# A two-layer transformer block on one core: layer two's queries and keys turned so that features lie on partitions, its output product from f16 parts

## What is computed

```
xn = layernorm(x)
x = x + attn0(xn) + ffn0(xn)     # 32 query heads of 8 over 8 key heads, causal, rotary; fp8 gated GELU, hidden 1024
xn = layernorm(x)
x = x + attn1(xn) + ffn1(xn)     # below; ternary weights, gated SiLU, rms norm, hidden 1024

def attn1(x):                    # 16 heads of 16; B=2, S=1024
    q, k, v = (x @ w.T).reshape(b, s, 16, 16) for w in (wq, wk, wv)
    q, k = apply_rope(q), apply_rope(k)       # pairs (even, odd) -> (x1 cos - x2 sin, x1 sin + x2 cos)
    scores = einsum('bshd,bstd->bsht', q, k) / 4      # among the 16 heads of ONE token
    attn = einsum('bsht,bstd->bshd', softmax(scores), v)
    return attn.reshape(b, s, 256) @ wo.T
```

## Time and profile before

| | |
|---|---|
| device time, median of 3 runs | 564.69 us (564.24 to 565.04) |
| the profiled execution | 564.45 us |
| its span in the trace | 562.7 us |
| mean granted clock of TensorE | 0.982 of full |
| busy: TensorE, its weight loads | 518.6 us (92%), 256.9 us |
| busy: ScalarE, VectorE, GpSimd | 468.0 (83%), 391.0 (69%), 234.7 us (42%) |
| DMA | 214396 packets, 46.05 MB; 40.5% of 16 engines' span on SP's queue |

### The profile page before, as it was taken

The page is one execution under the profiler, slowest core; times in us unless marked ns, Lnnn a source line. Parts: engine busy times, 40 slices in busy tenths (PEclk is TensorE's granted clock), DMA queues, the critical chain, the costliest instruction groups (busy, mean ns, idle before and its releaser), DMA issues.

```text
span 562.7 us, 12411 instructions
## 1 busy us (share of the span) xinstructions
PE 518.6 (92%) x4661; PEld 256.9 (46%) x4705; DVE 391.0 (69%) x845; ACT 468.0 (83%) x607; POOL 234.7 (42%) x302
## 2 busy tenths in 40 slices
PE   2489789999999999999999999999999999998885
PEld 1123334333444555545545454564454443455563
DVE  5756798977868678767788965748454455577673
ACT  2389999999999999999899889989898888963450
POOL 2576856443452257152765764044244210351100
PEclk9869999999999999999999999999999999999997
DMA  8923210311353516241421725455344253247853
GB/s 272 284 62 99 57 24 11 73 40 40 47 91 48 103 36 94 62 76 29 77 51 45 128 49 79 85 82 96 75 90 66 53 85 66 68 70 132 125 105 94
DMA packets 214396, 46.05 MB, mean 82 GB/s; under 512 B 197440, under 2 KB 213056, under 8 KB 214336
## 3 DMA queue, kind: packets, MB, share of 16 engines
q1 hardware_dynamic: 213760, 44.93, 40.5%
q10 hardware_dynamic: 576, 0.33, 0.4%
HBM read 19.02 MB, written 10.49 MB: 52 GB/s over the span
## 4 chain that ended last, share of the span: by engine, by line
PE 77%; DMA 6%; DVE 4%; ACT 4%; SPq 3%; issue 3%; POOL 2%; DVEq 0%; ACTq 0%
PE psV L706 23%; PE psS L692 8%; PE psA L875 3%; PE psC L782 3%; PE psS L828 3%; PE psC L875 3%; ACT Pt L958 2%; PE psB L875 2%; PE psB L885 2%; PE psA L885 2%; PE psB L839 2%; PE psA L782 2%; PE psA L743 2%; PE psB L743 2%; PE psC L743 1%
## 5 line engine op out<-in xcount | busy, mean ns | idle before, releaser
L958 ACT ACTIVATE Pt<-psS 128x1024 f32<-128x1024 f32 x288 | 280.1, 1031 | 24.0 <-PE psS L692 19.2
L706 PE MATMUL psV<-Pt,vaug 128*32 128x512 f32 x1152 | 149.8, 605 | 1.8 <-POOL Pt L1633 1.4
L1633 POOL TENSOR_SCALAR_AFFINE_SELECT Pt<-Pt 128x1024 f32<-128x1024 f32 x64 | 71.6, 1143 | 75.7 <-ACT Pt L958 75.5
L692 PE MATMUL psS<-qTf,kTf 32*128 32x512 f16 x576 | 65.8, 388 | 4.8 <-ACT Pt L958 3.1
L692 PEld LDWEIGHTS psS<-qTf,kTf 32*128 32x128 f16 x576 | 17.9, 91 | 84.2 <-ACT Pt L958 51.4
L1683 POOL TENSOR_TENSOR ss<-ss,mhalf 128x1 f32<-128x1 f32 x16 | 9.6, 597 | 87.0 <-DVE ss L1470 87.0
L706 PEld LDWEIGHTS psV<-Pt,vaug 128*32 128x32 f32 x1152 | 25.4, 108 | 42.7 <-issue 34.7
L1016 ACT ACTIVATE stage<-psS 128x1024 f32<-128x1024 f32 x32 | 31.0, 1023 | 7.0 <-PE psS L828 6.9
L1624 POOL TENSOR_TENSOR QXf<-rt,QXf 128x512 f16<-128x512 f32 x16 | 19.9, 1242 | 27.4 <-ACT QXf L945 27.4
L1304 DVE SCALAR_TENSOR_TENSOR gw<-gw,gb 128x512 f32<-128x512 f32 x32 | 27.6, 866 | 4.8 <-ACT gw L973 4.8
L1613 POOL TENSOR_TENSOR rt<-qkv,cs 128x320 f32<-128x320 f32 x16 | 16.1, 1003 | 27.4 <-DVE qkv L1189 19.8
(11 more groups left out here) (353 smaller groups left out, 1113.1 us busy)
## 6 DMA issues: line engine op xcount, KB each, us to landing
qkvscr<-rqkv SPq DMA_DIRECT2D x16, 384.0 KB, 2.7
G<-qkvscr SPq DMA_DIRECT2D x24, 128.0 KB, 3.8
stage<-in_wg SPq DMA_DIRECT2D x4, 512.0 KB, 8.2
w8g<-qkvscr SPq DMA_DIRECT2D x16, 128.0 KB, 3.6
oscr<-o SPq DMA_DIRECT2D x16, 128.0 KB, 3.2
at<-oscr SPq DMA_DIRECT2D x16, 128.0 KB, 2.5
out<-yout SPq DMA_DIRECT2D x16, 128.0 KB, 2.3
x<-in_x SPq DMA_DIRECT2D x1, 1536.0 KB, 12.3
```

The lines of the kernel that those rows point to most:

```text
L692: e.matmul(psS[j], kd[32 * j:32 * j + k, h, 128 * at:128 * at + 128], qd[32 * j:32 * j + k, 4 * h:4 * h + 4, :].rearrange("p s n -> p (s n ...
L706: ins = e.matmul(psV[32 * j:32 * j + 32, :], vaug[:, at, j, 32 * h:32 * h + 32], Pt[(4 * Q + j) % NP], start=(kb == 0 and h == 0), stop=(k ...
L958: e.activation(flat(Pt4[:, u % NP:u % NP + 2, :]), flat(psS4[:, j:j + 2, :]), ACT.Exp, scale=scale).then_inc(S["exp"], 1)
L1633: e.affine_select(out=p, in_=p, pattern=[[0, 8], [1, 128]], compare_op=ALU.is_ge, fill=0.0, base=0, channel_multiplier=-1).then_inc(S["mas ...
```

## The change

Queries and keys of layer two are computed with features on partitions, and stay so; the turn into groups goes through DRAM in the turned form.

- The columns of wq and wk are put in another order on the host (`turn`): first the even members of the rotary pairs of q and k, then the odd ones, each with (pair, head) as its 128 features. `qkv1.2n` has the weights as the stationary operand: 4 x 6 products of 128x128 weights with 128 tokens.
- The rotation takes tables with tokens along the free dimension (`turns`): `sin` writes them on ScalarE (two more activations of 1024 columns), `tT.0` to `tT.3` turn them on TensorE, `tTc.0` to `tTc.4` copy them. `rab` (DVE) multiplies straight from PSUM, `rr` (POOL) adds and subtracts. `qk1c`, `ro1`, `ro1p`, `ro2` leave the first pass.
- `rw` writes queries and keys to DRAM (two DMAs, runs of 8 values), `rd` reads them as S1 needs them (four DMAs of 16 partitions). The rows that hide other tokens are loaded once (`mk`). `gT`, `gTq`, `gTk` leave the first pass. `vw` and `vr` carry the values alone.
- `ow` writes in 1 KB runs, `at1r` gathers 64 B pieces. `a1p` (DVE) splits the result in f16 high and low parts, `aq` turns it by a DMA transpose, `wo1` is six f16 products of 256 columns. `at1T` and `at1Tc` leave the first pass; `yo` scales.
- The gating weights are loaded two to `stage`, two to `stmp`, the latter from ScalarE's queue; x from tile 4 on is loaded in three parts from there; the other weights follow later (`lc`, `lw`).
- Some buffers share one (`big`). The range checks take in the new values.
- All five lists of `ORDER` are new.

```diff
+            def mk(k):
+                w.wait_ge("tc", 0 if k else 12)
+                for s in range(2):
+                    dst = (qk1Todd if k else qk1T)[:, s, :, :].rearrange("p j n -> p (j n)")
+                    for b in range(4):
+                        e.dma_start(dst[32 * b + 16:32 * b + 24, :], A["ind2"][s]).then_inc(S[f"d_rd{k}"], 16)
+            def rw(n):
+                src = flat(rqkv[n % 2][:, 0:2, :]).rearrange("p (f m a) -> p f m a", f=2, a=8)
+                dst = rscr[n].rearrange("b s j (f i) (h a) -> f (i h) (b s j) a", f=2, a=8)
+                for f in range(2):
+                    w.wait_ge("rr", 2 * n + f + 1)
+                    e.dma_start(dst[f], src[:, f, :, :]).then_inc(S[f"d_rw{n % 2}"], 16)
+            def rd(n):
+                w.wait_ge(f"d_rw{n % 2}", 32 * (n // 2 + 1))
+                w.wait_ge(f"d_rd{n % 2}", 128)
+                w.wait_ge("S1", 4 * (n - 1))
+                for b in range(4):
+                    dst = (qk1Todd if odd(n) else qk1T)[32 * b:32 * b + 16, :, :, :].rearrange("p s j n -> p (s j) n")
+                    e.dma_start(dst, rscr[n, b].rearrange("s j d n -> d (s j) n")).then_inc(S[f"d_rd{n % 2}"], 16)
+            def aq(n):
+                w.wait_ge("a1p", 2 * n + 2)
+                w.wait_ge("wo1", n + 1 - len(at1q))
+                e.dma_start_transpose(at1q[n % len(at1q)], at1p).then_inc(S["d_aq"], 16)
...
+                    if part == 0:
+                        for c in range(4):
+                            for k, (pt, q, a) in enumerate(((0, 0, 0), (1, 0, 0), (0, 1, 0), (0, 0, 1), (1, 0, 1), (0, 1, 1))):
+                                ins = e.matmul(bank[:, 128 * c:128 * c + 128], wparts[:, q, a, 128 * c:128 * c + 128],
+                                               src[:, pt, 128 * a:128 * a + 128], start=(k == 0), stop=(k == 5))
+                        ins.then_inc(S["qkv1"], 1)
...
+                    for k, (pt, q, a) in enumerate(((0, 0, 0), (0, 1, 0), (0, 0, 1), (0, 1, 1), (1, 0, 0), (1, 0, 1))):
+                        ins = e.matmul(bank[:, 0:256], src[:, 2 * pt + a, :], wo1parts[:, q, a, :], start=(k == 0), stop=(k == 5))
+                    ins.then_inc(S["wo1"], 1)
...
+                e.activation(turns[:, 2, :].rearrange("p (m h) -> p m h", h=16),
+                             ang[:, 0, :].unsqueeze(2).to_broadcast([128, 64, 16]), ACT.Sin)
+                e.activation(turns[:, 1, :].rearrange("p (m h) -> p m h", h=16),
+                             ang[:, 2, :].unsqueeze(2).to_broadcast([128, 64, 16]), ACT.Sin, bias=hpi[:],
...
+            def rab(n):
+                bank = psM[filled["qkv1", 2 * n] % len(psM)][:].rearrange("p (e s t) -> p e s t", e=2, s=2)
...
+                for k in range(2):
+                    e.tensor_tensor(r1[:, k, :].rearrange("p (e s t) -> p e s t", e=2, s=2), bank,
+                                    turns[:, k:k + 2, t0:t0 + 128].unsqueeze(2).to_broadcast([128, 2, 2, 128]),
+                                    ALU.mult).then_inc(S["rab"], 1)
...
+                e.tensor_scalar(at1p[:, 0:256], at1[0][:], OUP, None, ALU.mult).then_inc(S["a1p"], 1)
+                w.wait_ge("a1p", 2 * n + 1)
+                e.scalar_tensor_tensor(at1p[:, 256:512], at1[0][:], OUP, at1p[:, 0:256], ALU.mult,
+                                       ALU.subtract).then_inc(S["a1p"], 1)
...
+            def rr(n):
+                dst = flat(rqkv[n % 2][:, 0:2, :])
+                w.wait_ge("rab", 2 * n + 2)
+                w.wait_ge(f"d_rw{n % 2}", 32 * (n // 2))
+                for f, op in enumerate((ALU.subtract, ALU.add)):
+                    e.tensor_tensor(dst[:, 256 * f:256 * f + 256].rearrange("p (b s j a) -> p s b j a", b=4, s=2, j=4),
+                                    by_group(r1[:, f, 0:256]), by_group(r1[:, f, 256:512]), op).then_inc(S["rr"], 1)
```

More of the change, by code:

```diff
@@ L191 @@
 QUAD_STAGES = {"pe": ("qk", "pv"), "act": ("exp",), "pool": ("mask",)}
-AGAIN = {"sp": [("wg", k) for k in range(6, 12)], "pool": [("zf", 0)] + [("w8a", k) for k in range(6)],
-         "dve": [step for k in range(6) for step in (("w8m", k), ("w8s", k))]}
+AGAIN = {"sp": [("wg", k) for k in range(6, 12)], "pool": [("zf", 0), ("gz2", 0)] + [("w8a", k) for k in range(6)],
+         "dve": [("cst", 0)] + [step for k in range(6) for step in (("w8m", k), ("w8s", k))]}
 def one_round(engine, n):
@@ L225 @@
     "wo0": lambda n: ("xa", n + 1), "up": lambda m: ("fh" if m % 2 else "g", m // 2 + 1), "down": lambda n: ("yff", n + 1), "flagT": lambda n: ("flag", 1), "wsum": lambda m: ("wmin", m + 1),
-    "xn1T": lambda n: ("xn1f", n - NT + 1), "qkv1": lambda m: ("v1c" if m % 2 else "qk1c", m // 2 + 1),
-    "gT": lambda m: ("gTk" if m % 2 else "gTq", m // 2 + 1), "gTagain": lambda n: ("gTm", n - NT + 1),
+    "xn1T": lambda n: ("xn1f", n - NT + 1), "qkv1": lambda m: ("v1c", m // 2 + 1) if m % 2 else ("rab", m + 2) if m < 2 * NT else ("qk1c", m // 2 - NT + 1),
+    "tT": lambda m: ("tTc", m + 1),
+    "gT": lambda m: ("gTk" if m % 2 else "gTq", m // 2 - NT + 1), "gTagain": lambda n: ("gTm", n - NT + 1),
     "PV1": lambda n: ("o1r", n + 1),
-    "o1T": lambda n: ("o1", 2 * n + 2), "at1T": lambda n: ("at1Tc", n + 1), "wo1": lambda n: ("yo", n + 1),
+    "o1T": lambda n: ("o1", 2 * n + 2), "at1T": lambda n: ("at1Tc", n - NT + 1), "wo1": lambda n: ("yo", n + 1),
     "gu": lambda m: ("hh" if m % 2 else "sg", m // 2 + 1), "dn1": lambda n: ("yout", n + 1),
@@ L257 @@
 idc vz tab cst w8 w8m w8s tsc tm tcs tw ln0 xn xnTc qkvc va wide q0 kl xs fTc rmax rcomb mxn mTc ob att attTc xa ge1 ge3 ge3b a8c yff
-wh wsq wsum ln1 xn1 xn1Tc xn1f wl wmin v1c ro1 ro2 gTq m1 gTm o1r o1 sg hh ssm hx at1Tc yo yout osum flag rng rngb
+wh wsq wsum ln1 xn1 xn1Tc xn1f wl wmin v1c tT tTc rab rr gTq m1 gTm o1r o1 sg hh ssm hx a1p at1Tc yo yout osum flag rng rngb
 zero gz zf rs0 rope ql mask ge4 xf rs1 ro1p rsg w8a""".split()
@@ L562, in all_landed @@
                     w.wait_ge(f"d_vw{p}", 16 * 8 * passes)
-                w.wait_ge("d_vr", 48 * NT * passes)
+                for p in range(2):
+                    w.wait_ge(f"d_vr{p}", read_back(NT * passes - 2 + p))
+                    w.wait_ge(f"d_rd{p}", 128 + 64 * 8)
                 w.wait_ge("d_ow", 16 * NT * passes)
@@ L566, in all_landed @@
                 w.wait_ge("d_ht", 16 * NT * passes)
[L568 to L575 removed]
+                w.wait_ge("d_aq", 16 * NT)
+            run = {"first": first, "lc": lc, "lw": lw, "mk": mk, "rw": rw, "rd": rd, "wg": wg, "wt": wt, "vw": vw, "vr": vr, "ow": ow, "at1r": at1r, "aq": aq, "out": out, "kt": kt, "qt": qt, "xt": xt, "ht": ht}
             ahead = e.mark_branch_hint_location()
@@ L818, in S1m, with tT @@
                             ins.then_inc(S["S1m"], 1)
+            def tT(m):
+                w.wait_ge("sin", 1)
+                w.wait_ge("d_id", 16)
+                bank = shared("tT", m)
+                for k in range(4):
+                    c0 = 512 * (m % 2) + 128 * k
+                    ins = e.transpose(bank[:, 128 * k:128 * k + 128], turns[:, 1 + m // 2, c0:c0 + 128], identf[:])
+                ins.then_inc(S["tT"], 1)
             def S1(n):
-                k = 24 if n < NT else 25
-                w.wait_ge("gTq", n + 1)
-                w.wait_ge("gTk", n + 1)
+                if n < NT:
+                    w.wait_ge(f"d_rd{n % 2}", 128 + 64 * (n // 2 + 1))
+                w.wait_ge("gTq", n - NT + 1)
+                w.wait_ge("gTk", n - NT + 1)
                 w.wait_ge("gTm", n - NT + 1)
@@ L1037, in hxa @@
                 e.activation(hx_b[:, 0, :], h1, ACT.Copy, scale=ss[n % len(ss)][:, 2:3]).then_inc(S["hxa"], 1)
-            run = {"wh": wh, "wsq": wsq, "qh": qh, "g": g, "hxa": hxa, "sin": sin, "tc": tc, "tde": tde, "exp": exp, "sq": sq, "fh": fh, "th": th, "qk1c": qk1c, "gTk": gTk, "ex1": ex1,
+            run = {"tTc": tTc, "wgx": wgx, "lx": lx, "wh": wh, "wsq": wsq, "qh": qh, "g": g, "hxa": hxa, "sin": sin, "tc": tc, "tde": tde, "exp": exp, "sq": sq, "fh": fh, "th": th, "qk1c": qk1c, "gTk": gTk, "ex1": ex1,
                    "tg": tg, "ssq": ssq}
@@ L1751 @@
     order = [((16 * f + 4 * r + h) * 8 + d) for f in range(2) for h in range(4) for r in range(4) for d in range(8)]
+    turn = [[16 * h + 2 * d + i for d in range(8) for h in range(16)] for i in range(2)]
     arrays = {
```

351 lines of the change are left out of this document (212 added, 139 removed), and 237 rows, old and new, of the table ORDER.

## The result

The changed kernel takes **583.9 us** (median of 4, 581.1 to 585.2) against 564.9: 1.034 times, interval 1.032 to 1.036. It is slower; I had predicted 547. The profiled execution is 581.1 us, its span 579.3. One of the seven runs of the kernel before that stand beside `e1` to `e4` took 991.9 us; it is left out of the ratios, and no trace shows why it was slow.

The account below looks back on a forecast made before the run. The prediction took TensorE, 77% of the span, as the main bound. From 564.45 us, -2 (first stage), +3 (second), -15.8 (third) and -3 (last) gave 546.65; with 0.24 for the median, 547 us, range 537 to 561.

Parts of the forecast that it names:

- the passage on the DMA queue: DMA queue, third stage: rw's small packets, 4.8 us of all 16 engines a tile, were to cost nothing there.
- The price of the packet: DMA queue: a 32 B packet of rw was priced like a 64 B one, 9.3 ns of one engine.
- the landing of one `rw`: Sign in the profile after: rw lands in 6 to 8 us; over 12 would speak for rival 2.
- rival 2: DMA engines, last stage: 32 B packets cost over twice the 64 B price; 561 at twice, 576 at three times; chance 0.12.
- the DMA share of the last stage: Sign in the profile after: the share of the DMA engines in the last stage stays below 0.95.
- -15.8: Third stage, 125 to 503.3 us: three quarters of 21.2 us less TensorE work come out of the time.
- the 2 us for SyncE's shorter queue: First stage, 0 to 29.5 us: less waiting in SyncE's queue saves 2 us, between +1 and -5.
- the 24 products: qkv1 on TensorE: 24 products of 128 columns take 1.32 us instead of 1.39, 1.0 us less over 14 tiles.
- Rival 3: TensorE, third stage: qkv1's 24 weight loads are not hidden, +13.4 us there; 561, or about 556; chance 0.08.
- the 8 us on tile 15's path: Last stage: rw and rd bring queries and keys sooner, so S1.15 may come 8 us sooner.
- the -3: Last stage, 503.3 us to the end: 3 of 8.8 us gained, between -9 and +10, the DMA engines being almost full.
- Rival 1: Third stage: ScalarE and order hold back half of the gain, nothing gained at the end; 555 us; chance 0.18.

Follow-up runs that it names:

- e1: The changed kernel with queries and keys written in runs of 128 B instead of 32 B, S1 reading with a stride of 4 values: 572.6 us.
- e4: The changed kernel with wo1 multiplying a constant tile, so that TensorE never waits for the transpose aq; 32 B writes stay: 577.1 us.
- e6: The changed kernel with 128 B runs instead of 32 B and S1 reading contiguous slices, regrouping left out, so the result is not computed: 556.4 us (0.985).

## Why the prediction was wrong

**The step that failed** is the passage on the DMA queue: "In the third stage this costs nothing: DMA is 0.40 busy, and between `qkv1` and its S1 stand 7 or more quads of over 3 us each. What waits behind SP's longer issues is `kt` and `qt`; they have the same distance." It looked at a mean share, at the write's own consumer, and at two of the transfers behind it. The transfers that were late are others, those with little distance: `at1r`, `aq`, `xt`, `ht`, and `rd` itself. In the third stage this costs 10.2 us (`e6` against after), where nothing was charged.

In the last stage the prediction did expect a cost: it laid 14 us of engine time on a share of 0.62, called the engines almost full, and kept 3 of 8.8 us. The packets cost 15.8 us there, of which 8.5 are TensorE's same matmuls taking longer; that the clock would fall behind the waits was not priced at all. Between the two profiled executions the packets cost 10.2 + 15.8 - 1.5 (ahead of quad 30) = 24.5 us; between the medians it is 27.5, of the 36.9 by which the forecast missed. Without them the kernel takes 556.4, 9.4 us above the forecast and inside the range.

**The price of the packet held.** I took 9.3 ns; a 32 B packet takes 8.2 on average. The pair lands in 8.4 us where 6.8 were reckoned. Of the signs named, the landing of one `rw` (6.9 us, forecast 6 to 8, rival 2 over 12) and the DMA share of the last stage (0.70, below 0.95) came out on the forecast's side while the kernel was slower, so neither was a sign of what went wrong. Rival 2 had the right sign and came near the size (576 at three times the price) by the wrong condition: it decided "from about 2.3 times on", and at 0.9 times the loss was there. It had only half of the place: 10.2 us of the loss lie in the third stage. The Trainium skill's rule behind it ("DMA: Bandwidth & Descriptors", Specifications: below 512 B a read-modify-write) doesn't tell 32 from 64 or 128 B. In the traces the packet takes 8.2, 10.3 and 13.2 ns at these sizes, without a jump between them; what happens at 512 B no run here shows.

**The terms**, with the packets out of the way (`e6`) and as measured (after). The forecast's stages were cut at 125 and 503.3 us, the measured ones at quad 30 and the last exponential:

| stage | forecast | `e6` | after |
|---|---|---|---|
| to the first exponential | -2 | +0.1 | +0.2 |
| to quad 30 | +3 | +3.1 | +1.5 |
| third | -15.8 | -11.2 | -1.0 |
| behind the last exponential | -3 | +0.1 | +15.9 |

- Start: the 2 us for SyncE's shorter queue did not come.
- Third stage: `e6` has two more `qkv1` steps in it, 1.44 + 0.67 = 2.1 us, so -13.3 of -15.8. One term was mis-sized: the 24 products were put at 1.32 us from `up`'s fp8 form; two starts give 493.09 - 491.65 = 1.44, 60 ns a product, +0.05 instead of -0.07 against the old 1.39.

```profile
491.65 1.51 PE L861 MATMUL psB<-xhs,wqkv 128*128 128x128 f16 x24
493.09 0.40 PE L765 MATMUL psS<-qTf,kTf 32*128 32x512 f16 x4
```

  Rival 3 is out: loads are hidden. The Trainium skill's 81 ns for a load and product pair ("TensorE: Matmul & The Clock Gate", Back-to-back issue gap) is above what this row shows. `wo1` steps 0.75 us instead of 0.66. By the same stepping, `gT` was 12.3 us, `at1T` 3.9 and the saving on `wo1` 2.8, less 0.7 for `qkv1`: 18.3 gone where I had 21.2, and 16.2 with the two steps more. 11.2 came. The other 5 us, and some 1.4 more for one `gu` and one `up` that the new list has outside this stage, I can't place in the rows; 29 matmul records of before are missing in this stage, which blurs just this sum. They stay open.
- Last stage: the 8 us on tile 15's path did come at 128 B, but they were no longer what the stage waits for. S1.15 stands 37.6 us behind the last exponential in `e6` and 45.1 before. Behind it the stage now ends by the feed-forward part: TensorE waits 7.3 us in three places for `ht`'s transposes, where before it waited for `at1r`. The term that was wrong is the -3: it was worked out on a chain that no longer ended last. In the kernel after, S1.15 stands 52.8 us behind the last exponential: nearly all that this stage loses to the packets, 15.2 us, is lost ahead of it.

```profile
525.68 1.17 PE L922 MATMUL psS<-kTf 24*128 24x128 f32 x32 [0.94 <-DMA kTf<-rscr]
...
528.88 2.67 PE L989 MATMUL psA<-wpT,stmp 128*128 128x256 bf16 x16 [2.02 <-DMA stmp<-qtmp]
...
547.05 3.52 PE L989 MATMUL psA<-wpT,stmp 128*128 128x256 bf16 x16 [4.48 <-DMA stmp<-qtmp]
```

- Rival 1 (ScalarE holds back) did not happen: in `e6` TensorE is busy 355.99 of the third stage's 356.60 us. I had named the order of the fillers as the thing most likely wrong; with the packets out of the way it was not.
